# Graph layer on one core: the bias b2 is added to x + h by GpSimd instead of VectorE

## The chip, the core and the metric

The kernel runs on one NeuronCore of a Trainium2 chip. The engines of that core work side by side and meet only at semaphores: TensorE (PE in the profile; PEld is its weight load), VectorE (DVE), ScalarE (ACT), GpSimd (POOL) and SyncE (SP). Sixteen DMA engines move data between the memory outside (HBM) and the on-chip memory (SBUF). TensorE writes its results to a second on-chip memory, PSUM. The metric is the device time of one execution, in microseconds (us).

## The reference, cut to what matters

The layer works on 6250 nodes of 256 features and 106250 edges of 96 features, the edges sorted by destination:

```python
h    = jnp.maximum(_layernorm(x, axis=-1), 0.0)
out1 = segment_sum(edge_attr, dst);  cnt = segment_sum(ones, dst)
out2 = segment_max(edge_attr, dst)         # 0 where cnt == 0
out3 = out1 / jnp.maximum(cnt, 1.0)
z    = jnp.concatenate([h, out1, out2, out3, u[0] for every node], axis=1)
y    = x + relu(z @ W1 + b1) @ W2 + b2 + h
```

W1 maps 608 inputs to 1024 hidden values, W2 maps these to 256. The part that the change touches is the sum x + h + b2, to which the product with W2 is added at the end.

## The kernel before, in words

**Tiles and batches.** A prologue computes, on the chip, where each node's edges begin, and orders the nodes by degree. The nodes then form 49 tiles of 128, one node on each partition, and these form 15 batches of 2, 3 or 4 tiles: batches 0, 1 and 14 have two tiles, batches 2 to 6 three, batches 7 to 13 four. The tiles of a batch belong to one or two *groups* with like numbers of edges.

**What happens to a batch.** GpSimd gathers the rows of x (line 301, into `xr`) and the edge rows (line 308, into one of two buffers, `ell`) by indirect DMA. ScalarE masks part of the edges (line 398). VectorE reduces the edges to sums and maxima in a tree of pairwise operations (lines 725 and 736; the functions `tree_head`, `tree_mid`, `tree_tail`); the last step of a tree writes `cat` and frees the edge buffer by the semaphore `tree_done`. ScalarE writes h into `cat` (line 419) and the means (lines 426 and 427). TensorE transposes `cat` (line 512). Since every fp32 value is split into a high and a low part, ScalarE writes the high part `inh` of the transposed tile and VectorE the low part `inl` (line 825). TensorE multiplies by W1 (lines 527, 531, 536) in eight chunks of 128 hidden values. Of each chunk ScalarE makes `hf` and `hh` (lines 407 and 409), VectorE `hl` (line 821), and TensorE multiplies these by W2 two chunks later (lines 547 and 551).

**x + h + b2.** `residual(b)` on VectorE adds h to `xr` (line 838), waits for that on the semaphore `dve_step`, and adds b2 (line 843, from `b2b`, which holds b2 on all partitions). Each of the two additions goes over two tiles at a time (128x512), or over one (128x256) where the batch has three. The last addition raises `xb_done`. `output(b)` on VectorE adds the product from PSUM (line 852), one and a half periods later; then GpSimd stores the rows (line 322, `scatter`).

**The order of the work** is written out by hand. The program of each engine is a loop over *periods* s = -1, 0, ... and eight steps m in each. In period s TensorE multiplies batch s, while batch s+1 is reduced and transposed, and data for batch s+2 are gathered. On VectorE, period s holds at m = 0 and 1 the tree of the first group of batch s+1, at m = 2 `output(s-1)` and the head of the second tree, at m = 3 and 4 the rest of that tree and `in_lo` of the tiles 0 and 1, at m = 5 `moments` of batch s+2, at m = 6 `in_lo` of tile 2 and then `residual(s+1)`, and at m = 7 `in_lo` of tile 3, `scales` of batch s+2 and the head of its first tree. TensorE's transposes stand behind the chunks m = 2, 3, 5 and 6, ScalarE's means at m = 2 and 5. GpSimd's period s is: the x rows of batch s+2, the edge gathers for the first group (each waits for the tree that frees its buffer), `scatter(s-1)`, the edge gathers for the second group.

Of the kernel before, what the change touches and what calls it, by code (L numbers as in the profile page):

```python
# [13 lines left out]
P = 128  # L14


def gnn_block(nc, x, dst, edge, u, W1, b1, W2, b2, out):
    f32, f32r, i32, bf16 = mybir.dt.float32, mybir.dt.float32r, mybir.dt.int32, mybir.dt.bfloat16
    ALU, ACT, AX = mybir.AluOpType, mybir.ActivationFunctionType, mybir.AxisListType

    N, D = x.shape
# [25 lines left out]
    NB = len(BATCHES)  # L47
# [15 lines left out]
    assert all(len(gs) <= 2 for gs in BATCHES)  # L63
    ELL, ES = 56, 26
    assert all(n * (k1 + k2) <= ELL and n * k2 <= ES for _, n, k1, k2, _, _ in groups)
    MASKED = 4
    assert all(k2 <= k1 or a < MASKED for a, _, k1, k2, _, _ in groups)
    KM = max(k2 for _, _, _, k2, _, _ in groups)
    XS = 4

    def width(b):
        return len(t_of[b])
# [15 lines left out]
    def part(q):  # L88

        w = 160 if q <= 8 else 232 if q <= 24 else 304  # L90
        return max(0, MEAN * q + STEP // 2 - w // 2), w
# [9 lines left out]
    def sbuf(name, shape, dt=f32):  # L101
        return nc.alloc_sbuf_tensor(name, shape, dt)
# [5 lines left out]
    b2b = sbuf("b2b", [P, D])  # L108
# [9 lines left out]
    xr = sbuf("xr", [P, XS, 4, D])  # L118
# [53 lines left out]
    def psum(name, shape):  # L172
# [6 lines left out]
    S = nc.alloc_semaphore  # L179
    consts, seam_free = S("consts"), S("seam_free")  # L180
    sd_in, seam_in, dstp_in, w1_in, w1r_in, w2_in, c_in, win_in = (S(n) for n in
        ("sd_in", "seam_in", "dstp_in", "w1_in", "w1r_in", "w2_in", "c_in", "win_in"))
# [6 lines left out]
    dve_step, dve_turn, mb_step, t1_step = S("dve_step"), S("dve_turn"), S("mb_step"), S("t1_step")  # L189
# [6 lines left out]
    h_done, outs_done, over_done, trans_done = S("h_done"), S("outs_done"), S("over_done"), S("trans_done")  # L196
    hiT_done, loT_done, rem_hi, rem_lo = S("hiT_done"), S("loT_done"), S("rem_hi"), S("rem_lo")
    l1_done, hi_done, lo_done, l2_done = S("l1_done"), S("hi_done"), S("lo_done"), S("l2_done")
    xb_done, evac_done = S("xb_done"), S("evac_done")
    g_in, g_used, g_upd, g_done, g_out, gt_in, gt_used = (S(n) for n in  # L200
        ("g_in", "g_used", "g_upd", "g_done", "g_out", "gt_in", "gt_used"))

# [16 lines left out]
    def evac_count(b, bank=1):  # L219

        return sum((width(c) + 1) // 2 for c in range(b)) + min(bank + 1, (width(b) + 1) // 2)

    def ybank(b, j):
        return yps[b % 2 * 2 + j // 2]
# [6 lines left out]
    with nc.Block() as block:  # L231
# [36 lines left out]
        def _(pool):  # L268
# [9 lines left out]
            for a, z in ((0, 9), (9, 25), (25, PER + 1)):  # L278
                w = part(z - 1)[1]
# [16 lines left out]
            def gather_x(b, ks_):  # L296
                if b >= XS and ks_[0] == 0:
                    pool.wait_ge(stored[b % XS], xs_count(b - XS))
                for k in ks_:
                    i = tiles[t_of[b][k]]  # L300
                    pool.indirect_dma_start(out=xr[:, b % XS, k, :], out_offset=None, in_=x,  # L301
                                            in_offset=bass.IndirectOffsetOnAxis(ap=nid[:, i:i + 1], axis=0)).then_inc(x_in[b % XS], 16)
# [8 lines left out]
            def gather_group(g):  # L311
                _, _, k1, k2, _, _ = groups[g]
                if g >= 2:
                    pool.wait_ge(tree_done, g - 1)
                gather_edges(g, idx1, 0, k1)
                gather_edges(g, idx2, k1, k2)

            def scatter(b):
                for k, t in enumerate(t_of[b]):
                    i = tiles[t]  # L320
                    pool.wait_ge(evac_done, evac_count(b, k // 2))
                    pool.indirect_dma_start(out=out, out_offset=bass.IndirectOffsetOnAxis(ap=oidx[:, i:i + 1], axis=0),  # L322
                                            in_=xr[:, b % XS, k, :], in_offset=None,
                                            bounds_check=N - 1, oob_is_err=False).then_inc(stored[b % XS], 16)

            pool.wait_ge(idx_ready, 1)
            gather_x(0, [0])
            pool.wait_ge(idx_ready, 2)
# [7 lines left out]
            def gather_general(g):  # L336
                a, n, _, _, _, _ = groups[g]
                with pool.If(general > 0):
                    pool.wait_ge(g_out, 48)
                    pool.wait_ge(gt_used, g)  # L340
                    for j in range(n):
                        for lo, size, rows in ((0, F, gsum), (F, F, gmax), (2 * F, 1, gcnt)):
                            pool.indirect_dma_start(out=gst[:, j, lo:lo + size], out_offset=None, in_=rows,
                                                    in_offset=bass.IndirectOffsetOnAxis(ap=nid[:, a + j:a + j + 1], axis=0)).then_inc(gt_in, 16)
# [4 lines left out]
            for s in range(-1, NB + 1):  # L349
                if s + 2 < NB:  # L350
                    gather_x(s + 2, list(range(width(s + 2))))
                for i, g in enumerate(g_of[s + 1] if s + 1 < NB else []):
                    if g + 1 < NG:
                        gather_general(g + 1)
                    if g == 0:
                        pool.wait_ge(w_lo, 4)
                    if g + 2 < NG:
                        gather_group(g + 2)
                    if i == 0 and s >= 1:
                        scatter(s - 1)  # L360
                if s + 1 >= NB:
                    scatter(s - 1)
            for i in range(XS):
# [209 lines left out]
        def _(dve):  # L573
            V = dve
            step = itertools.count(1)
# [4 lines left out]
                            in1=sd[0:SR, 0:SC].rearrange("p (r c) -> p r c", c=STEP)[:, :, 0:1].broadcast_to([SR, SPR, P]), op=ALU.is_gt).then_inc(coarse, 1)  # L580
# [27 lines left out]
            for i, q in enumerate(ON_DVE):  # L608
                lo, w = part(q)
# [84 lines left out]
            with dve.If(general > 0):  # L694
                V.memset(eT[F:F + 1, :], 1.0).then_inc(g_upd, 1)
                for p, (rows_, first, op) in enumerate(((F + 1, 0.0, ALU.add), (F, -FMAX, ALU.max))):
# [3 lines left out]
                    with dve.Fori(0, NROW) as r:  # L700
                        dve.wait_ge(g_in, r * 32 + (p * NROW * 32 + 32))
                        V.sem_inc(dve_turn, 1)
                        with dve.Fori(0, ROW) as j:
                            n = dve.value_load(gdst[0:1, bass.ds(j, 1)], min_val=0, max_val=N - 1)
# [127 lines left out]
            def residual(b):  # L832

                n = width(b)
                dve.wait_ge(h_done, t_of[b][-1] + 1)
                for j in range(0, n, 2):
                    w = min(2, n - j)
                    last = V.tensor_tensor(out=xr[:, b % XS, j:j + w, :], in0=xr[:, b % XS, j:j + w, :], in1=cat[:, j:j + w, 0:D], op=ALU.add)
                last.then_inc(dve_step, 1)
                dve.wait_ge(dve_step, next(step))  # L840
                for j in range(0, n, 2):
                    w = min(2, n - j)
                    last = V.tensor_tensor(out=xr[:, b % XS, j:j + w, :], in0=xr[:, b % XS, j:j + w, :], in1=b2b[:, None, :].broadcast_to([P, w, D]), op=ALU.add)
                last.then_inc(xb_done, 1)

            def output(b):
                n = width(b)
                dve.wait_ge(l2_done, (b + 1) * HC)
                dve.wait_ge(xb_done, b + 1)
                for j in range(0, n, 2):  # L850
                    w = min(2, n - j)
                    V.tensor_tensor(out=xr[:, b % XS, j:j + w, :], in0=ybank(b, j)[:, 0:w * D].rearrange("p (j d) -> p j d", d=D),  # L852
                                    in1=xr[:, b % XS, j:j + w, :], op=ALU.add).then_inc(evac_done, 1)
# [12 lines left out]
            for s in range(-1, NB + 1):  # L866
                b = s + 1
                n, gs = (width(b), g_of[b]) if b < NB else (0, [])
                for m in range(HC):
# [9 lines left out]
                    if m == 2:  # L879
                        if s >= 1:  # L880
                            output(s - 1)
                        if len(gs) > 1:
                            tree_head(gs[1])
# [11 lines left out]
                    if m == 6:  # L895
                        in_low(b, 2)
                        if n:
                            residual(b)
# [28 lines left out]
```

## Time and profile before

| | |
|---|---|
| time, median of 3 runs | 577.2 us (576.81 to 577.95) |
| profiled execution, its own time | 576.6 us |
| its span | 574.4 us |
| granted TensorE clock, mean over the span | 0.978 |
| PE busy | 481.2 us (84%) |
| DVE busy | 470.0 us (82%) |
| ACT busy | 351.0 us (61%) |
| POOL busy | 242.0 us (42%) |
| DVE line 843, the addition that the change moves | 27 instructions, 16.3 us |

"Busy" is the time in which an engine executes an instruction; matmuls are pipelined, so their rows overlap. Idle time in a row of the trace stands in brackets, with the engine and line that ended it. A time in a view counts from the start of the span.

### The profile page before, as it was taken

What the parts mean: (1) busy time and instruction counts of PE and PEld (TensorE: products, weight loads), DVE (VectorE), ACT (ScalarE), POOL (GpSimd) and SP (SyncE); (2) the same over time, 40 slices, a digit from 0 to 9 for tenths busy, and PEclk for the clock granted to TensorE, in tenths of its full rate; (3) what the DMA queues carried; (4) which work ended last, traced back from release to release, by engine and by line L of the source; (5) the groups of instructions that cost most, each with busy time, mean ns of one, the idle gap of its engine ahead of it and who ended that gap; (6) DMA issues with size and microseconds to landing.
All of it is one profiled execution on the core that took longest, in us unless ns stands there. A gap on an engine that the chain in (4) does not pass through costs nothing.

```text
span 574.4 us, 8775 instructions
## 1 busy us (share of the span) xinstructions
PE 481.2 (84%) x3016; PEld 443.3 (77%) x3016; DVE 470.0 (82%) x888; ACT 351.0 (61%) x951; POOL 242.0 (42%) x251
## 2 busy tenths in 40 slices
PE   0020569889999999877999999999999999999991
PEld 0020559889999899867988888888888888888991
DVE  4896768898998999989999998999989889793220
ACT  0934638676768586684856757667577685743330
POOL 2055430716182746645277274571752714202021
PEclk9999979898999999998999999999999999999997
DMA  2935430525253454733446245441550524001010
GB/s 79 287 97 172 139 132 2 171 100 181 100 165 142 152 182 141 246 105 126 157 147 212 70 137 193 151 167 66 184 199 15 158 90 156 34 0 38 1 38 18
DMA packets 18836, 71.12 MB, mean 124 GB/s; under 512 B 4571, under 2 KB 5755, under 8 KB 18776
## 3 DMA queue, kind: packets, MB, share of 16 engines
q0 software_dynamic: 15408, 65.72, 34.1%
q1 hardware_dynamic: 3378, 4.79, 2.8%
q8 instruction: 24, 0.39, 0.3%
q14 instruction: 26, 0.21, 0.1%
HBM read 64.09 MB, written 6.85 MB: 124 GB/s over the span
## 4 chain that ended last, share of the span: by engine, by line
PE 60%; DVE 15%; DMA 8%; ACT 7%; issue 5%; POOL 3%; SPq 0%; DVEq 0%; POOLq 0%; ACTq 0%
PE l1ps L527 24%; PE l1ps L531 12%; PE yps L547 11%; DVE work L736 9%; DMA work<-in_edge_attr,idx 6%; PE yps L551 6%; PE tps L512 3%; PE l1ps L536 3%; ACT work L398 3%; POOL work L308 2%; ACT cat L373 2%; DVE cat L736 1%; POOL out_y L322 1%; DMA work<-in_dst 1%; DVE inl L825 1%
## 5 line engine op out<-in xcount | busy, mean ns | idle before, releaser
L308 POOL DMA_INDIRECT work<-in_edge_attr,idx x98 | 118.4, 1208 | 202.5 <-DVE cat L736 153.3
L527 PE MATMUL l1ps<-inh,w1h 128*128 128x512 f32 (+2 forms) x480 | 173.8, 368 | 2.1 <-ACT hh L409 1.4
L527 PE MATMUL l1ps<-inh,w1l 128*128 128x512 f32 (+2 forms) x480 | 169.3, 359 | 0.0
L736 DVE TENSOR_TENSOR work<-work 128x768 f32<-128x768 f32 (+14 forms) x174 | 151.4, 902 | 1.1
L407 ACT ACTIVATE hf<-l1ps,b1e 128x512 f32<-128x512 f32 (+2 forms) x120 | 72.6, 605 | 108.2 <-PE l1ps L536 108.0
L398 ACT ACTIVATE work<-work,mk 128x96 f32<-128x96 f32 x435 | 122.5, 367 | 26.3 <-DMA work<-in_edge_attr,idx 26.0
L531 PE MATMUL l1ps<-inl,w1h 128*128 128x512 f32 (+2 forms) x480 | 112.9, 358 | 0.0
L821 DVE TENSOR_TENSOR hl<-hf,hh 128x512 fp32r<-128x512 f32 (+2 forms) x120 | 71.3, 594 | 42.8 <-ACT hh L409 37.1
L527 PEld LDWEIGHTS l1ps<-inh,w1h 128*128 128x128 f32 x480 | 92.7, 193 | 10.5 <-issue 2.0
L322 POOL DMA_INDIRECT out_y<-xr,oidx x49 | 68.3, 1393 | 77.1 <-DVE xr L852 63.0
L527 PEld LDWEIGHTS l1ps<-inh,w1l 128*128 128x128 f32 x480 | 93.0, 194 | 7.8
L547 PE MATMUL yps<-w2h,hh 128*128 128x256 f32 x392 | 98.5, 282 | 0.0
L547 PE MATMUL yps<-w2l,hh 128*128 128x256 f32 x392 | 98.1, 281 | 0.0
L531 PEld LDWEIGHTS l1ps<-inl,w1h 128*128 128x128 f32 x480 | 85.6, 193 | 10.3
L547 PEld LDWEIGHTS yps<-w2h,hh 128*128 128x128 f32 x392 | 74.3, 190 | 2.6
L547 PEld LDWEIGHTS yps<-w2l,hh 128*128 128x128 f32 x392 | 74.4, 190 | 2.4
L409 ACT ACTIVATE hh<-l1ps,b1e 128x512 fp32r<-128x512 f32 (+2 forms) x120 | 72.0, 600 | 0.0
L725 DVE TENSOR_TENSOR work<-work 128x1344 f32<-128x1344 f32 (+15 forms) x52 | 71.1, 1367 | 0.9
L551 PE MATMUL yps<-w2h,hl 128*128 128x256 f32 x392 | 66.2, 282 | 2.5 <-DVE hl L821 2.5
L301 POOL DMA_INDIRECT xr<-in_x,nid x49 | 51.3, 1047 | 36.1 <-DVE nid L643 21.5
L512 PE MATMUL tps<-ident,cat 128*128 128x128 f32 x196 | 31.3, 284 | 41.5 <-ACT cat L427 38.4
L512 PEld LDWEIGHTS tps<-ident,cat 128*128 128x128 f32 x196 | 22.7, 145 | 44.9 <-DVEq L786 34.5
(126 smaller groups left out, 478.5 us busy)
## 6 DMA issues: line engine op xcount, KB each, us to landing
work<-in_L_gnn_W SPq DMA_DIRECT2D x3, 1024.0 KB, 7.4
work<-in_edge_attr,idx POOLq DMA_INDIRECT x98, 5.3
xr<-in_x,nid POOLq DMA_INDIRECT x49, 4.0
out_y<-xr,oidx POOLq DMA_INDIRECT x49, 3.1
work<-in_dst SPq DMA_DIRECT2D x1, 415.0 KB
dstp<-in_dst SPq DMA_DIRECT2D x1, 415.0 KB
work<-in_L_gnn_W SPq DMA_DIRECT2D x3, 128.0 KB, 7.5
xr<-in_L_gnn_W SPq DMA_DIRECT2D x1, 256.0 KB, 11.1
```

The source lines that it names most:

```text
L308: pool.indirect_dma_start(out=ell[g % 2][:, at:at + kk * F], out_offset=None, in_=edge, in_offset=bass.IndirectOffsetOnAxis(ap=idx[:, a + ...
L322: pool.indirect_dma_start(out=out, out_offset=bass.IndirectOffsetOnAxis(ap=oidx[:, i:i + 1], axis=0), in_=xr[:, b % XS, k, :], in_offset=None,
L398: last = act.activation(es[g % 2][:, at * F:(at + 1) * F], ell[g % 2][:, src:src + F], ACT.Copy, scale=mk[:, a + j, e:e + 1])
L407: act.activation(hf[C % 2][:, 0:cols], l1ps[C % 2][:, 0:cols], ACT.Relu, bias=b1e[:, m:m + 1])
L409: act.activation(hh[C % 3][:, 0:cols], l1ps[C % 2][:, 0:cols], ACT.Relu, bias=b1e[:, m:m + 1]).then_inc(hi_done, 1)
L512: pe.transpose(tps[:, ks(c)], cat[:, k, ks(c)], ident[:, :])
L527: pe.matmul(ps, wt[:, c, ks(m)], inh[b % 2][:, c, 0:cols], start=(c == 0 and wt is w1h), stop=False)
L531: pe.matmul(ps, w1h[:, c, ks(m)], inl[b % 2][:, c, 0:cols], start=False, stop=False)
L547: pe.matmul(ybank(b, j)[:, j % 2 * D:(j % 2 + 1) * D], hh[C % 3][:, ks(j)], wt[:, m, :], start=(m == 0 and j % 2 == 0 and wt is w2h), stop ...
L551: last = pe.matmul(ybank(b, j)[:, j % 2 * D:(j % 2 + 1) * D], hl[C % 3][:, ks(j)], w2h[:, m, :], start=False, stop=(m == HC - 1), skip_gro ...
L736: return V.tensor_tensor(out=slots(buf, n, per, 0, size // 2) if out_ is None else out_, in0=slots(buf, n, per, 0, size // 2), in1=slots(b ...
L821: V.tensor_tensor(out=hl[C % 3][:, 0:cols], in0=hf[C % 2][:, 0:cols], in1=hh[C % 3][:, 0:cols], op=ALU.subtract).then_inc(lo_done, 1)
```

## The change

The second addition of `residual(b)` goes to a new function `bias2(b)` in GpSimd's program. GpSimd calls it at the end of its period s, for batch s: behind the second group's edge gathers, in front of the x gathers of the next period. `xb_done` is now raised by the addition of h, `bias2` waits for it and raises the new semaphore `b2_done`, and `output(b)` waits for that one. The wait on `dve_step` between the two additions goes too.

```diff
+            def bias2(b):
+
+                pool.wait_ge(xb_done, b + 1)
+                if b == 0:
+                    pool.wait_ge(c_in, 64)
+                for j in range(0, width(b), 2):
+                    w = min(2, width(b) - j)
+                    last = pool.tensor_tensor(out=xr[:, b % XS, j:j + w, :], in0=xr[:, b % XS, j:j + w, :], in1=b2b[:, None, :].broadcast_to([P, w, D]), op=ALU.add)
+                last.then_inc(b2_done, 1)
...
                     if i == 0 and s >= 1:
                         scatter(s - 1)
+                if s >= 0 and s < NB:
+                    bias2(s)
                 if s + 1 >= NB:
                     scatter(s - 1)
...
                     last = V.tensor_tensor(out=xr[:, b % XS, j:j + w, :], in0=xr[:, b % XS, j:j + w, :], in1=cat[:, j:j + w, 0:D], op=ALU.add)
-                last.then_inc(dve_step, 1)
-                dve.wait_ge(dve_step, next(step))
-                for j in range(0, n, 2):
-                    w = min(2, n - j)
-                    last = V.tensor_tensor(out=xr[:, b % XS, j:j + w, :], in0=xr[:, b % XS, j:j + w, :], in1=b2b[:, None, :].broadcast_to([P, w, D]), op=ALU.add)
                 last.then_inc(xb_done, 1)
 
             def output(b):
                 n = width(b)
                 dve.wait_ge(l2_done, (b + 1) * HC)
-                dve.wait_ge(xb_done, b + 1)
+                dve.wait_ge(b2_done, b + 1)
```

VectorE's program before, in the second half of period 1: the tail of `moments(3)`, `in_lo` of tile 2 of batch 2, `residual(2)` and the start of `scales(3)`.

```order
L799 TENSOR_SCALAR ve<-mv 128x3 [waits dve_step]
L821 TENSOR_TENSOR hl<-hf,hh 128x256 [waits l2_done,hi_done]
L825 TENSOR_TENSOR inl<-tps,inh 128x4x128 [waits hiT_done]
L830 TENSOR_TENSOR inr<-tpr,inr 32x384 [waits rem_hi]
L838 TENSOR_TENSOR xr<-xr,cat 128x512 [waits h_done]
L838 TENSOR_TENSOR xr<-xr,cat 128x256
L843 TENSOR_TENSOR xr<-xr,b2b 128x512 [waits dve_step]
L843 TENSOR_TENSOR xr<-xr,b2b 128x256
L821 TENSOR_TENSOR hl<-hf,hh 128x256 [waits l2_done,hi_done]
L804 RECIPROCAL r<-std 128x3 [waits std_ready]
```

The same place now (the lines of VectorE's program are numbered 7 or 12 higher):

```order
L811 TENSOR_SCALAR ve<-mv 128x3 [waits dve_step]
L833 TENSOR_TENSOR hl<-hf,hh 128x256 [waits l2_done,hi_done]
L837 TENSOR_TENSOR inl<-tps,inh 128x4x128 [waits hiT_done]
L842 TENSOR_TENSOR inr<-tpr,inr 32x384 [waits rem_hi]
L850 TENSOR_TENSOR xr<-xr,cat 128x512 [waits h_done]
L850 TENSOR_TENSOR xr<-xr,cat 128x256
L833 TENSOR_TENSOR hl<-hf,hh 128x256 [waits l2_done,hi_done]
L816 RECIPROCAL r<-std 128x3 [waits std_ready]
```

The two additions of b2 and their wait are gone, and nothing else has moved. The same holds in each of the 15 batches.

GpSimd's program before, where period 2 ends and period 3 begins (`work` holds the edge buffers; `stored1` says that the old rows of this `xr` slot are out):

```order
L308 DMA work<-in_edge_attr,idx 128x1728 [waits tree_done]
L308 DMA work<-in_edge_attr,idx 128x1344
L301 DMA xr<-in_x,nid 128x256 [waits stored1]
L301 DMA xr<-in_x,nid 128x256 x2
L338 COMPARE_AND_BRANCH
```

The same place now:

```order
L308 DMA work<-in_edge_attr,idx 128x1728 [waits tree_done]
L308 DMA work<-in_edge_attr,idx 128x1344
L333 TENSOR_TENSOR xr<-xr,b2b 128x512 [waits xb_done]
L333 TENSOR_TENSOR xr<-xr,b2b 128x256
L301 DMA xr<-in_x,nid 128x256 [waits stored1]
L301 DMA xr<-in_x,nid 128x256 x2
L348 COMPARE_AND_BRANCH
```

The additions of batch 2 stand behind the edge gathers of this period, and the x gathers of the next period stand behind the additions.

## Rows read from the trace of the kernel before

**Rows 1.** Busy time in two stretches: us, then busy us (instructions) of each engine.

```profile
79.00:280.00 201.00, 184.31 (x1235) 181.56 (x1236) 180.35 (x342) 140.01 (x404) 97.59 (x82) 0.97 0.45 150
280.00:560.00 280.00, 279.45 (x1672) 246.18 (x1671) 229.48 (x362) 174.64 (x445) 115.92 (x93) 1.00 0.31 106
```

**Rows 2.** TensorE in order of time: start, us, instructions, [idle before, released by].

```profile
79.11 1.09 PE L512 MATMUL tps<-ident,cat 128*128 128x128 f32 x4 [3.04 <-ACT cat L427]
101.76 0.63 PE L512 MATMUL tps<-ident,cat 128*128 128x128 f32 x4 [2.18 <-ACT cat L427]
129.11 0.63 PE L512 MATMUL tps<-ident,cat 128*128 128x128 f32 x4 [2.08 <-ACT cat L427]
170.94 0.63 PE L512 MATMUL tps<-ident,cat 128*128 128x128 f32 x4 [0.47 <-ACT cat L427]
188.89 0.63 PE L512 MATMUL tps<-ident,cat 128*128 128x128 f32 x4 [0.44 <-ACT cat L427]
201.22 0.63 PE L512 MATMUL tps<-ident,cat 128*128 128x128 f32 x4 [0.81 <-ACT cat L427]
219.29 0.63 PE L512 MATMUL tps<-ident,cat 128*128 128x128 f32 x4 [0.61 <-ACT cat L427]
232.53 0.63 PE L512 MATMUL tps<-ident,cat 128*128 128x128 f32 x4 [1.68 <-ACT cat L427]
252.94 0.63 PE L512 MATMUL tps<-ident,cat 128*128 128x128 f32 x4 [1.93 <-ACT cat L427]
268.72 0.63 PE L512 MATMUL tps<-ident,cat 128*128 128x128 f32 x4 [2.97 <-ACT cat L427]
306.06 0.63 PE L512 MATMUL tps<-ident,cat 128*128 128x128 f32 x4 [0.43 <-ACT cat L427]
```

**Rows 3.** VectorE in order of time, batches 0 to 2, same columns.

```profile
68.10 0.69 DVE L843 TENSOR_TENSOR xr<-xr,b2b 128x512 f32<-128x512 f32 x1
...
90.86 0.42 DVE L821 TENSOR_TENSOR hl<-hf,hh 128x256 fp32r<-128x256 f32 x1 [0.49 <-ACT hh L409]
...
114.77 0.69 DVE L825 TENSOR_TENSOR inl<-tps,inh 128x512 fp32r<-128x512 f32 x1 [1.34 <-ACT inh L434]
115.49 0.56 DVE L830 TENSOR_TENSOR inr<-tpr,inr 32x384 fp32r<-32x384 f32 x1
116.08 1.03 DVE L838 TENSOR_TENSOR xr<-xr,cat 128x512 f32<-128x512 f32 x2
117.14 1.03 DVE L843 TENSOR_TENSOR xr<-xr,b2b 128x512 f32<-128x512 f32 x2
118.08 0.42 DVE L821 TENSOR_TENSOR hl<-hf,hh 128x256 fp32r<-128x256 f32 x1
...
127.84 0.36 DVE L736 TENSOR_TENSOR cat<-work 128x192 f32<-128x192 f32 x1
```

**Rows 4.** VectorE's first idle time after residual(6).

```profile
247.42 0.56 DVE L821 TENSOR_TENSOR hl<-hf,hh 128x384 fp32r<-128x384 f32 x1 [1.47 <-issue]
```

**Rows 5.** The chain that ended last: two equal chunks of TensorE: start, us.

```profile
129.84 2.55 PE l1ps L527 x8
132.40 1.10 PE l1ps L531 x4
...
135.28 1.39 PE l1ps L527 x8
136.67 0.69 PE l1ps L531 x4
```

**Rows 6.** GpSimd in order of time, end of period 1, and a gather in period 5.

```profile
112.71 0.96 POOL L308 DMA_INDIRECT work<-in_edge_attr,idx  x1 [0.30 <-issue]
113.98 0.95 POOL L301 DMA_INDIRECT xr<-in_x,nid  x1 [0.30 <-issue]
...
128.47 0.94 POOL L308 DMA_INDIRECT work<-in_edge_attr,idx  x1 [10.89 <-DVE cat L736]
...
220.10 2.81 POOL L308 DMA_INDIRECT work<-in_edge_attr,idx  x1 [0.30 <-DVE xr L852]
```

**Rows 7.** VectorE beside that last gather.

```profile
219.94 2.15 DVE L725 TENSOR_TENSOR work<-work 128x1920 f32<-128x1920 f32 x1
```

**Rows 8.** GpSimd's iota, line 277.

```profile
L277 POOL IOTA ident<- x1: 232/232/232, 1.5 to 1.5; 128x128 f32 x1
```

**Rows 9.** Waits of VectorE from 280 to 560 us: total, times, longest.

```profile
DVE hl L821 <- ACT hh L409: 29.8, 14, 3.8
DVE inl L825 <- ACT inh L434: 13.9, 13, 1.9
```

More of the change, by code:

```diff
@@ L198, in gnn_block @@
     l1_done, hi_done, lo_done, l2_done = S("l1_done"), S("hi_done"), S("lo_done"), S("l2_done")
-    xb_done, evac_done = S("xb_done"), S("evac_done")
+    xb_done, b2_done, evac_done = S("xb_done"), S("b2_done"), S("evac_done")
     g_in, g_used, g_upd, g_done, g_out, gt_in, gt_used = (S(n) for n in
```

## The prediction

> **What bounds the kernel now.** I read the busy times of two stretches first [rows 1]. From 280 to 560 us TensorE is busy for 279.45 of 280 us, so nothing that VectorE saves there can shorten the run. From 79 to 280 us TensorE is busy for 184.31 of 201 us: 16.7 us are idle, and VectorE is busy for 180.35. Before 79 us lies the prologue. So the gain must come from the first half.
>
> Then I read TensorE's idle times one by one [rows 2]. The reader is to see that nearly all of them end with ScalarE's means (line 427), which wait for the last step of a tree on VectorE. Behind each I followed VectorE back to its own last idle time, because a saving counts only if VectorE doesn't wait between the removed instruction and the tree's end. In period 1 to 2 VectorE waits 1.34 us before `in_lo` at 114.77 and then runs without a gap past `residual(2)` up to the tree's end at 127.84 [rows 3]; TensorE follows at 129.11. That pattern (a wait before `in_lo` of tile 2, then `residual`, then no gap up to the trees of the next period) comes back after residuals 3, 4 and 5. The chain of waits often enters at ScalarE's `hh` in these places, but VectorE was still busy with the instruction before, so its own work was the limit there.
>
> **The change part by part.** *Removed from VectorE:* 27 instructions of line 843. A pair of 128x512 and 128x256 takes 1.03 us, with the gap before it 1.06 us [rows 3]; the single one of batch 0 takes 0.69, with its gap 0.71. I take 1.06 for each batch of three tiles and some 1.3 for four.
>
> What of it reaches TensorE, batch by batch:
> - Residual 0 (68.10 us): VectorE runs through to the tree that TensorE waits 3.04 us for at 79.11. Gain 0.71 us.
> - Residual 1 (period 0): VectorE waits 0.49 us for ScalarE right behind it, at 90.86 [rows 3]. It is paced by TensorE here; gain 0.
> - Residual 2: TensorE's wait of 2.08 us at 129.11 becomes 1.02. Gain 1.06 us.
> - Residual 3: only 0.47 us of idle time is left in that period (170.94). Gain 0.47.
> - Residual 4: waits of 0.44 and 0.81 us (188.89, 201.22), together 1.25. Gain 1.06.
> - Residual 5: 0.61 and 1.68 us (219.29, 232.53). Gain 1.06.
> - Residual 6: VectorE waits 1.47 us at 247.42 [rows 4], because ScalarE is held by masks that wait for gathered edges. TensorE's waits of 1.93 and 2.97 us (252.94, 268.72) come down from there. Gain 0.
> - Residual 7: 0.43 us at 306.06. Gain 0.43. The other residuals lie where TensorE is never idle: 0.
>
> The sum is 0.71 + 1.06 + 0.47 + 1.06 + 1.06 + 0.43 = 4.8 us.
>
> *The clock.* After the waits of 2.18, 2.08 and 2.97 us TensorE was granted less than its full 2.4 GHz for a while. At 129.84 the eight and four matmuls of a chunk take 2.55 and 1.10 us, at 135.28 the same take 1.39 and 0.69 [rows 5]: 1.57 us lost. After 1.93 us no such loss follows. If the wait at 129.11 falls to 1.02 us, this loss may go as well: 0 to 1.6 us. The nearest waits without a loss speak for the upper end; that the waits may regroup speaks against it. I take 0.7.
>
> *Added to GpSimd:* 27 additions. No row shows one on this engine. Below, it takes what VectorE needs, 0.69 us for 128x512 [rows 3]. Above, I take the longest GpSimd instruction of the periods, 2.81 us [rows 6]. The nearest row for how it computes is the iota: 128 elements in 0.232 us, at most 1.8 ns each [rows 8], so 512 elements at 0.93 us or less for one stream. Two inputs make it longer; I take 1.2 us, and 0.6 for one tile, so 2.1 us for a pair with a gap of 0.3.
>
> The Trainium skill has a price for this: GPSIMD Engine Reference, section "Performance versus the Vector engine", measures an fp32 addition of 2048 elements at 4497 ns against VectorE's 2293. A quarter of it is an estimate of 1.12 us; by it the pair is 2.0 us and the sum stays as it is. No row here shows it.
>
> *What is queued behind it.* On GpSimd the x gathers of the next period come 2 to 3 us later. They are issued from 113.98 us, and GpSimd then idles 10.89 us until 128.47 [rows 6]; their data are read by `moments` a period later, so this costs nothing. The edge gathers of the second group stand ahead of the additions, those of the next period behind that idle time. `output(b)` waits for `b2_done` only some ten us or more after the additions. Cost 0; if the cover were gone, each us late would be one us of VectorE.
>
> *What they share.* Does a GpSimd addition slow VectorE? Gathers take 0.95 us where VectorE idles or reads PSUM, but 2.81 us at 220.10 [rows 6], beside an instruction of line 725 that starts at 219.94 and lasts 2.15 us [rows 7]. Something is shared, and GpSimd gives way. The reverse isn't to be seen. If it exists, its price depends on where the additions fall. In period 1 they start at 113.98 us. VectorE idles until 114.77 and then reads PSUM for `inl` and `inr` until 116.08: 2.1 us of cover, as long as the pair. In the 4-tile periods they fall beside `residual` and `hl`, with VectorE's waits of 29.8 and 13.9 us around them [rows 9]. In periods 4 and 5 a few tenths overlap. I charge 0.3 us in all. Below, it is 0: all nine additions of periods 1 to 5 find cover. Above stands the slower rival.
>
> The sum: 4.8 + 0.7 - 0.3 = 5.2 us. From the profiled execution's 576.6 that is 571.4; the median of the runs shown is 0.6 above that execution, so I forecast 572.0 us.
>
> **Rivals.**
>
> *A: GpSimd's additions hold VectorE up (slower).* For it: the 2.81 us gather shows that the two engines meet somewhere, and most of VectorE's trees read two tiles of SBUF. Against it: the cover at 113.98 to 116.08. Price: if cover doesn't help, VectorE loses 1.8 us per pair of three tiles and saves 1.06, +0.74; over the four periods after residuals 2 to 5 that is +3.0, less 0.71 of batch 0: 579.5 us. With the upper end (2.81 and 1.4 us, 4.5 with a gap) and the cover of 2.1 us, it loses 2.4 and saves 1.06: 4 x 1.34 - 0.71 = +4.7, 581.9 us. Middle 580.5. It decides from a pair longer than 2.1 + 1.06 = 3.2 us, or without cover from 1.06 us.
>
> Beside it stands a rule of the Trainium skill, SBUF — State Buffer, section "Who interferes with whom": a VectorE instruction with two SBUF inputs and a GpSimd instruction that reads SBUF exclude each other, and whichever starts first blocks the other in full. By this rule an instruction with an input in PSUM isn't blocked, which is the cover above. The trace agrees in one direction only (the 2.81 us).
>
> *B: no gain.* The freed time turns into waits on ScalarE's masks and the edge DMAs, as after residual 6, or on TensorE's pace, as after residual 1. For it: both patterns exist, and 43.7 us of VectorE's idle time in the second half are waits of that kind. Against it: five of the batches in the first half show no such wait. Only batch 0's 0.71 us stays: 576.5 us.
>
> *C: more gain.* The slow clock after 129 us goes in full (1.6), and the one after 268.72 as well, by about 1.1 us (an estimate: two thirds of the loss in rows 5), and half of the waits there, 1.0: 4.8 + 1.6 + 1.1 + 1.0 = 8.5: 568.7 us.
>
> **How the numbers follow.** The forecast 0.66 (its own range 570 to 574), A 0.11, B 0.12, C 0.11. The range for 8 in 10: low 569.0, which cuts half of C, and high 577.5, which takes in B and leaves A out. A measurement of this kernel can tell about 0.2%, 1.15 us. Faster: forecast and C, 0.77. Same: B, 0.12. Slower: A, 0.11.
>
> **What would show it.** In the changed kernel's trace: VectorE's busy time down by about 16 us; the wait at 129 us near 1 us and no stretched chunk behind it; TensorE's idle time from 79 to 280 us down from 16.7 to some 12 to 13 us; `residual` followed at once by `hl`; 27 GpSimd additions near 1.2 us, and the rows of lines 725 and 736 as long as before. Wrong would be: additions on VectorE that are longer than 1.03 us per pair beside GpSimd's, GpSimd additions over 2 us, or gathers that start later after a tree's end than before.

## The result, and the profile after

Median of six runs each, in turn on the same chip: 577.58 us before (576.81 to 578.24), 575.53 us after (575.11 to 576.79). The ratio is 0.9969, with a 95% interval of 0.9955 to 0.9982. The kernel became faster by 0.31%, 1.8 us, where 5.2 us had been forecast. The profiled execution of the changed kernel was the slowest of its six (576.79 us, span 575.0), that of before, at 576.6 us (span 574.4), was faster than each of its six, so the two spans don't show the gain. Where the time went has to be read inside them.

Busy time of each engine in the whole span, after:

```profile
PE 483.4 (84%) x3016; PEld 445.6 (77%) x3016; DVE 479.4 (83%) x861; ACT 350.2 (61%) x951; POOL 272.5 (47%) x278
```

VectorE executes 27 instructions fewer, and yet its busy time is up, from 470.0 to 479.4 us. The forecast had it down by 16. So some 25 us were added to instructions that nobody edited. The same in the two stretches of [rows 1]:

```profile
79.00:280.00 201.00, 187.31 (x1245) 184.91 (x1246) 182.58 (x331) 142.95 (x413) 112.90 (x94) 0.95 0.45 150
280.00:560.00 280.00, 277.80 (x1657) 244.11 (x1657) 237.00 (x347) 171.21 (x437) 131.54 (x108) 1.00 0.32 105
```

From 79 to 280 us TensorE's idle time falls from 16.7 to 13.7 us, where the forecast had 12 to 13. From 280 to 560 us it rises from 0.55 to 2.20 us: TensorE now waits in the half in which it hardly ever did. VectorE's busy time there is up by 7.5 us although additions have left it.

The added instructions, by form (count, busy us, mean ns, idle time ahead of them):

```profile
L333 POOL TENSOR_TENSOR xr<-xr,b2b 128x512 f32<-128x512 f32 x22 | 28.2, 1297 | 9.0 <-DVE xr L850 8.8
L333 POOL TENSOR_TENSOR xr<-xr,b2b 128x256 f32<-128x256 f32 x5 | 4.2, 850 | 0.0
```

GpSimd's addition takes 1.30 us where 1.2 had been taken, so the size of the addition was not the mistake. VectorE in a period with a batch of four tiles (512 columns of `hl`), in order of time:

```profile
307.53 0.69 DVE L837 TENSOR_TENSOR inl<-tps,inh 128x512 fp32r<-128x512 f32 x1 [0.88 <-ACT inh L446]
308.14 4.34 DVE L850 TENSOR_TENSOR xr<-xr,cat 128x512 f32<-128x512 f32 x2
312.40 0.68 DVE L833 TENSOR_TENSOR hl<-hf,hh 128x512 fp32r<-128x512 f32 x1
```

and GpSimd beside it:

```profile
307.81 0.95 POOL L308 DMA_INDIRECT work<-in_edge_attr,idx  x1 [0.30 <-issue]
308.78 2.54 POOL L333 TENSOR_TENSOR xr<-xr,b2b 128x512 f32<-128x512 f32 x2
311.48 1.25 POOL L301 DMA_INDIRECT xr<-in_x,nid  x1 [0.16 <-issue]
```

The same place in the kernel before:

```profile
309.91 1.28 DVE L838 TENSOR_TENSOR xr<-xr,cat 128x512 f32<-128x512 f32 x2
311.23 1.29 DVE L843 TENSOR_TENSOR xr<-xr,b2b 128x512 f32<-128x512 f32 x2
312.44 0.68 DVE L821 TENSOR_TENSOR hl<-hf,hh 128x512 fp32r<-128x512 f32 x1
```

GpSimd comes to the additions of a batch behind the gathers of the period, with no idle time ahead of them, and by then VectorE is at the residual of the next batch (line 850), which reads two tiles of SBUF. The pair took 1.28 us and takes 4.34: 3.05 us lost, where moving b2 saved 1.29. Nearly all of it lies in the first of the two additions at line 850: by its record it takes 3.74 us, the second 0.68. The 3.05 us are more than the 2.54 us of GpSimd's pair. The first addition began at 308.14 and needs 0.68 us; it would have been over at 308.82, when GpSimd's addition has only just begun in the records (308.78). At 346.19 and 384.13 us the same pair has 3.05 us too much again; at 422.15 us it has 2.72 and at 461.03 us 1.66.

GpSimd's pair for batch 12 (491.13 to 493.69 us) falls on another place, the last steps of a tree. After, and the same steps before:

```profile
488.84 5.28 DVE L748 TENSOR_TENSOR work<-work 128x384 f32<-128x384 f32 x4
```

```profile
489.37 2.27 DVE L736 TENSOR_TENSOR work<-work 128x384 f32<-128x384 f32 x4
```

These 3.01 us stand right ahead of the end of the tree, and TensorE's longest wait of the second half follows (0.90 us at 495.69, below).

It doesn't happen everywhere. VectorE in period 2:

```profile
143.62 0.69 DVE L837 TENSOR_TENSOR inl<-tps,inh 128x512 fp32r<-128x512 f32 x1 [0.73 <-ACT inh L446]
144.34 0.56 DVE L842 TENSOR_TENSOR inr<-tpr,inr 32x384 fp32r<-32x384 f32 x1
144.93 1.03 DVE L850 TENSOR_TENSOR xr<-xr,cat 128x512 f32<-128x512 f32 x2
```

with GpSimd's addition of the same time:

```profile
143.02 2.00 POOL L333 TENSOR_TENSOR xr<-xr,b2b 128x512 f32<-128x512 f32 x2
```

GpSimd adds from 143.02 to 145.02 us, and VectorE isn't slowed: it idles first, and then `inl` and `inr`, whose first input lies in PSUM, take what they took before (0.69 and 0.56, [rows 3]). This was the cover of the forecast, and it holds in periods 2 to 4. In period 1, where the batch has a single addition, that one met an `hl` at 114.54 (1.84 us long, own length 0.42), in periods 5 and 6 the pair met the residual (2.51 us long at 233.48, where 0.68 is its own).

TensorE's waits, the rows that answer to [rows 2], and three of the second half:

```profile
79.41 1.09 PE L524 MATMUL tps<-ident,cat 128*128 128x128 f32 x4 [3.33 <-ACT cat L439]
102.84 0.63 PE L524 MATMUL tps<-ident,cat 128*128 128x128 f32 x4 [2.18 <-ACT cat L439]
114.04 0.63 PE L524 MATMUL tps<-ident,cat 128*128 128x128 f32 x4 [2.45 <-ACT cat L439]
199.18 0.63 PE L524 MATMUL tps<-ident,cat 128*128 128x128 f32 x4 [0.70 <-ACT cat L439]
229.69 0.63 PE L524 MATMUL tps<-ident,cat 128*128 128x128 f32 x4 [1.64 <-ACT cat L439]
250.00 0.63 PE L524 MATMUL tps<-ident,cat 128*128 128x128 f32 x4 [1.96 <-ACT cat L439]
265.79 1.09 PE L524 MATMUL tps<-ident,cat 128*128 128x128 f32 x4 [2.97 <-ACT cat L439]
...
304.30 0.63 PE L524 MATMUL tps<-ident,cat 128*128 128x128 f32 x4 [0.45 <-ACT cat L439]
...
371.28 0.63 PE L524 MATMUL tps<-ident,cat 128*128 128x128 f32 x4 [0.38 <-DVE inl L837]
447.32 0.63 PE L524 MATMUL tps<-ident,cat 128*128 128x128 f32 x4 [0.29 <-DVE inl L837]
495.69 0.63 PE L524 MATMUL tps<-ident,cat 128*128 128x128 f32 x4 [0.90 <-ACT cat L439]
```

The transposes that began at 306.06 us before begin at 304.30 now, 1.76 us earlier, although this execution reached its first transposes 0.59 us later (60.87 against 60.28; the kernel before, profiled again further down, has 60.77). The last three rows are waits of the second half that before hasn't. The wait of 2.08 us at 129.11 is gone, but one of 2.45 us at 114.04 stands ahead of it, with the slow chunk behind it (from the chain that ended last; at 118.55 the same work with a granted clock of 1.00):

```profile
114.78 1.65 PE l1ps L539 x8
116.43 0.85 PE l1ps L543 x4
...
118.55 0.94 PE l1ps L539 x8
119.49 0.47 PE l1ps L543 x4
```

### The profile page after: what moved, and what is told of

Its sections match the earlier page's. It is cut to its first block, busy times and chain, and to the rows that moved or that the text cites. A ratio compares the mean times of both kernels' runs of the same rounds, so it can differ in the third digit from the quotient of the medians.

```text
span 575.0 us, 8776 instructions
## 1 busy us (share of the span) xinstructions
PE 483.4 (84%) x3016; PEld 445.6 (77%) x3016; DVE 479.4 (83%) x861; ACT 350.2 (61%) x951; POOL 272.5 (47%) x278
## 4 chain that ended last, share of the span: by engine, by line
PE 58%; DVE 12%; DMA 8%; ACT 8%; issue 6%; POOL 6%; SPq 0%; POOLq 0%; DVEq 0%; ACTq 0%
PE l1ps L539 23%; PE l1ps L543 12%; PE yps L559 11%; DVE work L748 8%; DMA work<-in_edge_attr,idx 6%; PE yps L563 5%; PE tps L524 3%; POOL work L308 3%; ACT work L410 3%; PE l1ps L548 3%; POOL out_y L322 3%; ACT cat L385 2%; DMA work<-in_dst 1%; DVE cat L748 1%; ACT hf L419 1%
## 5 line engine op out<-in xcount | busy, mean ns | idle before, releaser
L308 POOL DMA_INDIRECT work<-in_edge_attr,idx x98 | 114.1, 1164 | 179.2 <-DVE cat L748 133.0
L748 DVE TENSOR_TENSOR work<-work 128x768 f32<-128x768 f32 (+14 forms) x174 | 154.5, 919 | 1.1
L833 DVE TENSOR_TENSOR hl<-hf,hh 128x512 fp32r<-128x512 f32 (+2 forms) x120 | 76.2, 635 | 41.5 <-ACT hh L421 36.6
L301 POOL DMA_INDIRECT xr<-in_x,nid x49 | 53.3, 1087 | 34.5 <-DVE nid L655 21.7
```

Source lines behind the costliest of these rows:

```text
L308: pool.indirect_dma_start(out=ell[g % 2][:, at:at + kk * F], out_offset=None, in_=edge, in_offset=bass.IndirectOffsetOnAxis(ap=idx[:, a + ...
L748: return V.tensor_tensor(out=slots(buf, n, per, 0, size // 2) if out_ is None else out_, in0=slots(buf, n, per, 0, size // 2), in1=slots(b ...
L833: V.tensor_tensor(out=hl[C % 3][:, 0:cols], in0=hf[C % 2][:, 0:cols], in1=hh[C % 3][:, 0:cols], op=ALU.subtract).then_inc(lo_done, 1)
```

## The experiments

The theory after the result, HOLD in the expectations: a GpSimd addition reads SBUF, and a VectorE instruction with two inputs in SBUF waits for it. What the forecast's sum gained is real, and the hold takes part of it. Its rivals: the gross sum was too high (SMALL); GpSimd is merely busy, so its gathers are late (QUEUE); it is the writing that disturbs. The ratios are to the kernel before on the same chip, with the 95% interval in brackets; behind each stands the median in us.

**b2 nowhere.** The addition is left out on both engines, so the output lacks b2.

```diff
-                if s >= 0 and s < NB:
-                    bias2(s)
...
-                dve.wait_ge(b2_done, b + 1)
+                dve.wait_ge(xb_done, b + 1)
```

> b2 is added by no engine (the output lacks b2); all else is as after the change. Theory HOLD: a GpSimd addition holds up every VectorE instruction with two SBUF inputs until it ends, and that eats most of what the removed additions are worth. Then this kernel shows the whole worth, the 4.8 to 6.4 us of the prediction: 571.2 to 572.8 us where the kernel before takes 577.6. Theory SMALL: the removed additions were worth only 2 us from the start. Then it takes 575.5, as after the change.

Measured: 0.9926 [0.9911, 0.9942], 573.47 us.

```profile
PE 479.9 (84%) x3016; PEld 442.7 (78%) x3016; DVE 454.0 (80%) x861; ACT 351.1 (62%) x951; POOL 238.2 (42%) x251
```

VectorE is busy for 454.0 us, 16.0 less than before. This is the ceiling of the change: 0.74%, 4.3 us (of 578.19). The forecast had 5.5 us for it, 4.8 gross and 0.7 from the clock. The changed kernel stays 0.43% above, some 2.5 us, and that is the price of GpSimd's additions; with the two intervals it is known to about 1.2 us either way.

**Writing without reading.** The additions give place to iotas (instructions that write a counting pattern and read no tile) of about the same total length in the same places. They write the tile that held b2, which nothing reads any more; b2 isn't added.

```diff
-                    last = pool.tensor_tensor(out=xr[:, b % XS, j:j + w, :], ...)
+                    for _ in range(2 * w):
+                        pool.wait_ge(wr_step, wr[0])
+                        wr[0] += 1
+                        last = pool.iota(b2b[:, :], pattern=[[1, D]], ...).then_inc(wr_step, 1)
...
```

> b2 is added by no engine; in place of each GpSimd addition stand iotas of 256 elements (four for 128x512, two for 128x256), which write SBUF and read none and keep GpSimd busy for about as long (4 x 0.3 us with gaps). Theory HOLD (it is the reading that holds VectorE up): as without b2, within 0.6 us of e1_drop, no VectorE instruction stretched. Theory QUEUE (the time in GpSimd's queue delays gathers and stores): as after the change, 575.5 us.

Measured: 0.9921 [0.9905, 0.9936], 573.39 us. GpSimd's iotas by form, and eight of them in the place of the pair above:

```profile
L338 POOL IOTA b2b<- 128x256 f32 x98 | 34.1, 348 | 13.9 <-DVE xr L856 8.1
```

```profile
307.92 3.25 POOL L338 IOTA b2b<- 128x256 f32 x8
```

VectorE beside them:

```profile
307.29 1.28 DVE L856 TENSOR_TENSOR xr<-xr,cat 128x512 f32<-128x512 f32 x2
308.55 0.69 DVE L839 TENSOR_TENSOR hl<-hf,hh 128x512 fp32r<-128x512 f32 x1
```

GpSimd is occupied for as long (34.1 us against 32.4) in the same places, and line 856, the residual, keeps its 1.28 us. Neither a busy GpSimd nor its writes cost anything that shows. What costs is something that the addition does and the iota doesn't, and the theory names it: it reads SBUF. No run has a GpSimd instruction that reads and doesn't write.

**Both engines add.** VectorE's second addition comes back and GpSimd's stays; b2 is added twice.

```diff
                 last.then_inc(dve_step, 1)
+                dve.wait_ge(dve_step, next(step))
+                for j in range(0, n, 2):
+                    last = V.tensor_tensor(... in1=b2b ...)
```

> Both engines add b2 (the output holds it twice): VectorE as before the change, GpSimd as after. So nothing is saved and only the price of the GpSimd additions shows. HOLD: VectorE loses 2 to 3 us in most batches, and the time is 577.6 plus 3 to 5 us: 580.5 to 582.5. SMALL: the price is near nothing, 577.6 to 578.2.

Measured: 1.0206 [1.0189, 1.0223], 590.3 us, 12 us more than before, where 3 to 5 were expected, and far more than the price of 2.5 us. The price isn't a constant. The likely reading is that in the changed kernel VectorE's saved 16 us absorb much of the 25.4 us of stretch (479.4 less 454.0). Here VectorE has 27.9 us of stretch (497.9 less 470.0) and nothing saved, and from 280 to 560 us TensorE is idle for 9.5 us, against 0.55 before:

```profile
280.00:560.00 280.00, 270.53 (x1569) 234.88 (x1568) 248.05 (x363) 170.39 (x437) 134.36 (x107) 1.00 0.32 106
```

**Halves.** GpSimd adds b2 for some batches, VectorE for the others.

```diff
+    ON_POOL = [7, 8, 9, 10, 11, 12, 13, 14]   # or [0 .. 6], or [2, 3, 4, 5]
...
-                if s >= 0 and s < NB:
+                if s in ON_POOL:
                     bias2(s)
...
```

> GpSimd adds b2 for batches 7 to 14 only, VectorE for 0 to 6 as before. HOLD: in this half nothing is to be gained since TensorE never idles before, and the stretched VectorE instructions make it late: 577.6 + 1.5 to 2.5 = 579.1 to 580.1 us. SMALL or QUEUE with free time in that half: 577.6.

> GpSimd adds b2 for batches 0 to 6, VectorE for 7 to 14 as before. Theory HOLD (a GpSimd addition holds up VectorE instructions with two SBUF inputs; in the first half most of that falls into VectorE's waits, in the second it makes TensorE wait): if the two halves add up, this is after (-0.3%) less second half (+0.46%) = -0.77% against before, 573.5 us where before takes 578. If the gain of the whole change lay elsewhere, it is 575.5 to 578.

> GpSimd adds b2 for batches 2 to 5 only: those whose additions find cover in the trace after the change, or whose delay ends in a wait for masks. HOLD: it keeps the 1.06 + 0.47 + 1.06 + 1.06 us of the prediction and part of the clock loss, loses 0.7 of batch 0 and spares the held instructions of batches 0, 1 and 6: -3.5 to -4.5 us, 573.5 to 574.5 where before takes 578.

Measured: second half alone 1.0046 [1.0029, 1.0064], 580.76 us; first half alone 0.9940 [0.9926, 0.9955], 574.9 us; batches 2 to 5 alone 0.9937 [0.9916, 0.9958], 574.97 us. Moving the additions of batches 7 to 14 makes the kernel slower than not moving them at all, by 2.7 us (0.46% of 578.19). The first half alone was expected at 573.5 us and stays short of that. Its gain lies in batches 2 to 5 as far as the intervals tell; for their residuals the forecast had 3.65 us, and 0.63% is 3.6 (2.4 to 4.9 by the interval).

The same can be read inside the traces, free of what one execution has ahead of it: from the transposes near 306 us to those near 495, two rows of TensorE in each trace. In the one with the second half alone:

```profile
307.76 0.63 PE L525 MATMUL tps<-ident,cat 128*128 128x128 f32 x4 [0.43 <-ACT cat L440]
...
499.82 0.63 PE L525 MATMUL tps<-ident,cat 128*128 128x128 f32 x4 [0.85 <-ACT cat L440]
```

Read in this way from each trace:

| kernel | from | to | us |
|---|---|---|---|
| before | 306.06 | 495.17 | 189.11 |
| b2 nowhere | 302.54 | 491.61 | 189.07 |
| iotas | 303.44 | 492.53 | 189.09 |
| first half alone | 307.22 | 496.27 | 189.05 |
| batches 2 to 5 alone | 304.91 | 493.96 | 189.05 |
| after | 304.30 | 495.69 | 191.39 |
| second half alone | 307.76 | 499.82 | 192.06 |

Without additions on GpSimd in this stretch it takes 189.1 us whatever else is changed; with them, 2.3 to 2.95 us more. That is where the larger part of the missing gain went.

**The additions moved to where VectorE waits.** GpSimd waits for the `hl` of a later chunk of the period before it adds, so that the pair falls on VectorE's waits and its PSUM reads; the additions of batches 5 and 14 stay where they were. Everything is computed.

```diff
                 pool.wait_ge(xb_done, b + 1)
+                if b == 0:
+                    pool.wait_ge(lo_done, 3)
+                elif b < 5:
+                    pool.wait_ge(lo_done, b * HC + 6)
+                elif 6 <= b <= 13:
+                    pool.wait_ge(lo_done, b * HC + 7)
```

> All b2 additions stay on GpSimd, but each waits for a point in VectorE's program behind which VectorE idles or reads PSUM: the hl of chunk m = 2 (batch 0), of chunk 5 (batches 1 to 4), of chunk 6 (batches 6 to 13). HOLD: the stretched instructions go from about 23 us in sum to under 8, and the time is near that without b2: 573.5 to 574.5 where before takes 578. If an addition holds VectorE up whatever its place: 575.5, as after. A second question: after the change the held instruction waits already 0.64 us before the addition's recorded start, while the gather in front of it is still running. If the hold begins when the addition is queued, not when it starts, an addition that is released by a semaphore with GpSimd idle holds nothing before its recorded start.

> Batches 0 to 6 on GpSimd with the same waits as in e7_timed, 7 to 14 on VectorE as before. HOLD: at least as good as e5_first_half, by the held instructions of periods 0, 1 and 6 (0.4 to 1.5 us): 572.5 to 573.5 where before takes 578.

The second is the first with `ON_POOL = [0 .. 6]`. Measured: all batches 0.9928 [0.9914, 0.9943], 574.43 us; first half 0.9920 [0.9906, 0.9934], 573.63 us. With the same 27 additions on GpSimd as in the changed kernel, the gain more than doubles, and the intervals of the two ratios (0.9914 to 0.9943, 0.9955 to 0.9982) don't meet. The first kernel's busy times:

```profile
PE 482.2 (84%) x3016; PEld 444.8 (78%) x3016; DVE 456.8 (80%) x861; ACT 351.2 (61%) x951; POOL 282.6 (49%) x278
```

VectorE is 2.8 us above its time without b2, where the changed kernel was 25.4 above. One pair of GpSimd, and VectorE beside it:

```profile
348.93 2.54 POOL L339 TENSOR_TENSOR xr<-xr,b2b 128x512 f32<-128x512 f32 x2 [2.97 <-DVE hl L839]
```

```profile
348.09 0.69 DVE L839 TENSOR_TENSOR hl<-hf,hh 128x512 fp32r<-128x512 f32 x1 [1.30 <-ACT hh L427]
349.98 0.69 DVE L843 TENSOR_TENSOR inl<-tps,inh 128x512 fp32r<-128x512 f32 x1 [1.20 <-ACT inh L452]
350.71 0.69 DVE L848 TENSOR_TENSOR inr<-tpr,inr 32x512 fp32r<-32x512 f32 x1
...
352.52 1.55 DVE L743 TENSOR_TENSOR work<-work 128x1344 f32<-128x1344 f32 x1
```

From 348.93 to 351.47 us VectorE idles and reads PSUM, and nothing is stretched. The stretch from 306 to 495 us takes 189.07 us again (305.20 to 494.27). The kernel with the first half moved and timed is the fastest that computes everything, 0.80% under before, where the changed one is 0.31% under it. Whether it is faster than its sibling with all batches the runs don't tell: the two intervals overlap.

**The additions moved onto the trees.** The counter-test: those of batches 0 to 12 wait for the last small step of the layer norm (`ln_done`), behind which VectorE starts a tree.

```diff
+                if b + 2 < NB:
+                    pool.wait_ge(ln_done, b + 3)
```

> All additions on GpSimd as after the change, but those of batches 0 to 12 wait for the last instruction of VectorE's scales (semaphore ln_done), behind which the head of the next tree starts at once: two long additions with both inputs in SBUF, and no idle time. GpSimd is idle when it is released, so no gather stands in front. HOLD: VectorE loses the pair's length of 2.0 to 2.6 us in nearly every batch with nothing to cover it, against 1.06 to 1.38 us saved, so the run is slower than before: 580 to 585 us where before takes 578. If the hold depends on the gather in front, or if GpSimd gives way to an instruction that VectorE has begun and then runs without holding it, 573.5 to 575.5.

Measured: 1.0150 [1.0123, 1.0176], 585.85 us. With the same additions this kernel is 7.5 us slower than the one before by the medians (1.5% of 578.34 is 8.7), where in the best places they gain 4. VectorE at a tree's head, and GpSimd:

```profile
120.27 3.33 DVE L739 TENSOR_TENSOR work<-work 128x1344 f32<-128x1344 f32 x2
123.63 0.42 DVE L835 TENSOR_TENSOR hl<-hf,hh 128x256 fp32r<-128x256 f32 x1
```

```profile
120.50 2.48 POOL L335 TENSOR_TENSOR xr<-xr,b2b 128x512 f32<-128x512 f32 x1 [5.46 <-DVE off L828]
...
357.71 5.04 POOL L335 TENSOR_TENSOR xr<-xr,b2b 128x512 f32<-128x512 f32 x2 [5.33 <-DVE off L828]
```

Here VectorE was in its instruction first (at 120.27; the pair took 2.34 us before, 3.33 now), and GpSimd's addition takes 2.48 us instead of 1.30. By the single records VectorE's first instruction keeps its 1.55 us and its second takes 1.74 where some 0.8 is its own: GpSimd waits for the first, and the second waits for GpSimd. So the engines exclude each other in both directions. The sum of VectorE's stretch doesn't set the time: it is 20.7 us here (474.7 less 454.0) and 25.4 us in the changed kernel, which is about 10 us faster. Part of the loss may come from x gathers that start late behind the waiting additions; this wasn't taken apart.

**The kernel before again**, with nothing changed.

> The kernel before, unchanged, timed against itself. It tells how far a ratio near 1 strays, and whether the 0.6 us by which TensorE's first transposes come later in the profiled execution after the change (60.87 against 60.28 us, before anything that the change touches) is a difference between executions or between programs. Both theories: ratio 1.000 within 0.2%. If it is between executions, the first transposes of this profile lie anywhere from 60.2 to 61.2 us.

Measured: 1.0003 [0.9993, 1.0012], 578.21 us. TensorE in its trace:

```profile
114.26 0.63 PE L512 MATMUL tps<-ident,cat 128*128 128x128 f32 x4 [2.30 <-ACT cat L427]
...
130.91 0.63 PE L512 MATMUL tps<-ident,cat 128*128 128x128 f32 x4 [0.56 <-ACT cat L427]
```

The same code has its long wait at 114.26 us in this execution, where [rows 2] have it at 129.11 with 2.08 us. A wait like that of the changed kernel at 114.04 thus comes without the change too, and the forecast's use of the one at 129.11 rested on a single execution.

## Why the prediction was wrong in size

The direction and the mechanism of the gain were right: 1.8 us faster. The size was off by 3.4 us (5.2 forecast). Of these, 1.2 us were missing from the gain (5.5 forecast for gross and clock together, 4.3 measured without b2), and 2.2 us lie in the price of GpSimd's additions (0.3 forecast, 2.5 measured). By its own steps:

- *Gross gain of 4.8 us.* Near. Without b2 anywhere 4.3 us are gained, and batches 2 to 5 alone gain 3.6 (forecast 3.65), both with whatever the clock gave back. The entry of 1.06 us for residual 2 can be seen: where the additions are replaced by iotas, made for batches 2 to 5 alone, or moved in time, the wait near 129 us is 1.01 us (forecast 1.02). Not every entry was right: batch 0's 0.71 us went in part to a wait of 0.42 us for a mask at 70.25, and a `hl` was held at 80.41 (2.16 us long, own length 0.42).
- *The clock, 0.7 us.* Not borne out. The row behind it was of one execution; after the change a slow chunk stands at 114.78 us, and it costs 1.1 us (2.50 against 1.41) where the one at 129.84 had cost 1.57. From 79 to 280 us the granted clock was 0.97 before and 0.95 after. No run sets the clock's part apart.
- *A GpSimd addition takes 1.2 us, a pair 2.1.* Right: 1.30, and 2.00 to 2.54 for a pair.
- *What is queued behind it, 0.* Right as far as the iotas show: about the same delay to the same gathers, and 0.9921.
- *What they share, 0.3 us "in all".* **This is the step that failed.** The price is 2.5 us (0.43% between the changed kernel and the one without b2). In the traces 2.3 us stand in one stretch, from 306 to 495 us. The forecast had written that "in the 4-tile periods they fall beside `residual` and `hl`, with VectorE's waits of 29.8 and 13.9 us around them", and took 0 for it. The trace it had contradicts that: the waits stand around the residual, not under GpSimd's pair. In the kernel before, GpSimd comes to the x gathers, the place of the additions, while VectorE is in the residual that began at 309.91:

```profile
310.83 1.19 POOL L301 DMA_INDIRECT xr<-in_x,nid  x1 [0.30 <-issue]
```

In the worst periods a pair loses 3.05 us and saves 1.3, VectorE then has 1.8 us less to spare, and in some of them TensorE waits for it. For the first half, where the 0.3 us were meant, the cover held in three of five periods; timing the additions there brought 0.9920 against 0.9940, some 1.2 us, though the intervals overlap.

- *"TensorE is busy for 279.45 of 280 us, so nothing that VectorE saves there can shorten the run."* Right, and it misled: what VectorE loses there can lengthen it. The forecast's sum has gains from the second half (0.43 us) and no losses.
- *Rival A* (580.5 us) had the mechanism, and applied it to the periods after residuals 2 to 5, where most of the cover held, instead of to the 4-tile periods. The changed kernel is the forecast's first half with rival A's mechanism in the second. The halves measured apart, -0.60% and +0.46%, give -0.14%; together -0.31% were measured, and the three intervals, each about 0.15% to either side, allow both.

The rule that the forecast quoted from the Trainium skill, SBUF — State Buffer, section "Who interferes with whom", is borne out here in most of its points: two SBUF inputs are held, a PSUM input isn't (143.62 us), and the one that starts first blocks the other (120.27 us). By the records 308.14 us goes against the last point: VectorE's instruction starts 0.64 us ahead of GpSimd's and is the one that waits. Applied place by place, the rule would have put a loss of about a pair's length on the 4-tile periods, where the forecast had none.

Left open: why the hold begins ahead of the recorded start of an addition that is queued behind a gather (0.6 us at 308.14), or whether the record starts late. The gather alone doesn't hold: in the kernel before, one from 309.57 to 310.52 us stands beside the residual at 309.91, which keeps its 1.28 us. The additions of the timed kernel meet next to no reader of two SBUF tiles, and those on the trees were released while VectorE was already running, so neither tells.

## What to carry over

Work moved from VectorE to GpSimd is not off VectorE if it reads SBUF: the same additions gave -0.7%, -0.3% or +1.5% of the time by nothing but what they waited for. Place them with a wait where the other engine idles or reads PSUM, and move only those whose saving reaches the bounding engine. And where an engine has no slack to give, price the losses there as carefully as the gains elsewhere.

## What the runs showed of the hardware

- A 128x512 fp32 addition takes 1.30 us on GpSimd and 0.69 on VectorE; 128x256 takes 0.74 to 0.77 in four of five records, against 0.42 (the fifth, 1.25 us, stands beside VectorE's residual). An iota of 128x256 takes 0.348 us, while the program's own of 128x128 took 0.232 [rows 8].
- Two GpSimd additions that follow one another leave VectorE no gap between them: a residual addition of 0.68 us waited for both (3.74 us long by its record at 308.14).
- Two executions of one program differ in where TensorE's long waits and slow clock fall (114 or 129 us): 2.08 us at 129.11 in one, 2.30 us at 114.26 and 0.56 at 130.91 in the other. A stretch without such a wait (306 to 495 us) repeats within 0.06 us over seven kernels that don't add on GpSimd there, or add where VectorE waits.
